# DLRM tower on one core: the last MLP layer as 64-wide parts on both halves of TensorE

## The reference

```
e = stack([tbl_f[ids[:, f]] for f in range(32)], axis=1)          # 1024 x 32 x 16
xk = e
for W in (W0, W1, W2):
    xk = relu(einsum('bmd,bhd,mhk->bkd', e, xk, W))               # 1024 x 64 x 16
    outs.append(sum(xk, axis=2))                                  # 1024 x 64
h = concatenate(outs + [dense_ctx], axis=1)                       # 1024 x 208
h = maximum(h @ W_top1 + b_top1, 0)                               # 1024 x 512
h = maximum(h @ W_top2 + b_top2, 0)                               # 1024 x 256
y = h @ W_top3                                                    # 1024 x 1
```

## Time and profile before

| | |
|---|---|
| median of 3 runs | 623.99 us (623.82 to 624.78) |
| the profiled execution, own time | 625.95 us |
| its span, first to last instruction | 624.0 us |
| TensorE busy | 600.8 us (96%) |
| VectorE, ScalarE, GpSimd busy | 515.1 (83%), 322.4 (52%), 444.2 us (71%) |
| granted TensorE clock, mean | 0.997 |

### The profile page before, as it was taken

The page is one execution under the profiler, slowest core; times in us unless marked ns, Lnnn a source line. Parts: engine busy times, 40 slices in busy tenths (PEclk is TensorE's granted clock), DMA queues, the critical chain, the costliest instruction groups (busy, mean ns, idle before and its releaser), DMA issues.

```text
span 624.0 us, 8470 instructions
## 1 busy us (share of the span) xinstructions
PE 600.8 (96%) x2926; PEld 211.4 (34%) x2926; DVE 515.1 (83%) x454; ACT 322.4 (52%) x545; POOL 444.2 (71%) x346
## 2 busy tenths in 40 slices
PE   4779899999999999999999999999999999999998
PEld 3532333333333333333333333333333333333454
DVE  0258698999989998999899998999899999888500
ACT  1333565555565454565545554545565456643564
POOL 6778858788787878787887878786878875556300
PEclk9999999999999999999999999999999999999999
DMA  4597787867887777677767887777667868750000
GB/s 128 184 333 257 283 308 292 285 239 258 274 283 274 258 244 253 222 289 246 258 227 282 283 275 245 252 283 253 222 236 265 289 242 273 269 197 0 1 1 0
DMA packets 45199, 144.49 MB, mean 232 GB/s; under 512 B 9619, under 2 KB 24085, under 8 KB 32870
## 3 DMA queue, kind: packets, MB, share of 16 engines
q1 hardware_dynamic: 36966, 141.85, 62.8%
q0 software_dynamic: 8192, 2.11, 4.0%
HBM read 139.21 MB, written 4.72 MB: 231 GB/s over the span
## 4 chain that ended last, share of the span: by engine, by line
PE 87%; POOL 5%; DMA 5%; issue 2%; SPq 1%; ACT 0%
PE acc L677 77%; POOL gathered L506 5%; PE x_ps L672 5%; DMA x_rows<-gathered 3%; PE sums_ps L746 2%; PE x_ps L746 2%; DMA gathered<-in_table,idx 1%; SPq L419 0%; DMA x_wide<-x_rows 0%; SPq L408 0%; DMA base_sb<-in_base 0%; PE sums_ps L672 0%; POOL idx L529 0%; ACT x_wide L593 0%; ACT x_wide L596 0%
## 5 line engine op out<-in xcount | busy, mean ns | idle before, releaser
L627 DVE TENSOR_TENSOR dve_ring<-x_wide,x_ps 128x1024 f32<-128x1024 f32 x428 | 489.2, 1215 | 62.2 <-issue 47.2
L677 PE MATMUL acc<-dve_ring,w_sb 128*64 128x512 f32 (+1 forms) x1744 | 474.6, 589 | 6.8 <-DVE dve_ring L627 6.8
L506 POOL DMA_INDIRECT gathered<-in_table,idx x256 | 243.8, 952 | 69.7 <-issue 64.1
L518 POOL TENSOR_TENSOR pool_ring<-x_wide,x_sb 128x1024 f32<-128x1024 f32 x84 | 199.3, 2383 | 76.7 <-ACT x_sb L577 46.9
L677 PEld LDWEIGHTS acc<-dve_ring,w_sb 128*64 128x64 f32 x1744 | 150.9, 138 | 293.4 <-issue 268.6
L677 PE MATMUL acc<-pool_ring,w_sb 128*64 128x512 f32 x336 | 131.6, 592 | 0.0
L567 ACT ACTIVATE x_ps<-acc 64x512 f32<-64x512 f32 (+1 forms) x132 | 73.5, 557 | 110.5 <-PE acc L677 108.2
L677 PE MATMUL acc<-pair_squares,w_sb 128*64 128x512 f32 (+1 forms) x264 | 113.9, 581 | 1.2 <-ACT pair_squares L547 1.2
L577 ACT COPY x_sb<-layer_out 64x512 f32<-64x512 f32 x128 | 79.0, 617 | 3.6
L547 ACT ACTIVATE pair_squares<-x_ps 128x1024 f32<-128x1024 f32 x32 | 32.8, 1025 | 88.5 <-PE sums_ps L672 88.2
L572 ACT ACTIVATE layer_out<-acc 64x512 f32<-64x512 f32 (+1 forms) x98 | 56.8, 579 | 2.4 <-PE acc L677 1.0
(11 more groups left out here) (36 smaller groups left out, 127.1 us busy)
## 6 DMA issues: line engine op xcount, KB each, us to landing
x_wide<-x_rows SPq DMA_DIRECT2D x96, 1024.0 KB, 8.0
x_wide<-x_rows SPq DMA_DIRECT2D x32, 768.0 KB, 5.6
x_wide<-x_rows SPq DMA_DIRECT2D x32, 256.0 KB
gathered<-in_table,idx POOLq DMA_INDIRECT x256, 4.5
x_rows<-gathered SPq DMA_DIRECT2D x32, 128.0 KB
w_sb<-in_w SPq DMA_DIRECT2D x2, 512.0 KB, 5.7
x_rows<-gathered SPq DMA_DIRECT2D x32, 16.0 KB
x_wide<-in_W_top SPq DMA_DIRECT2D x1, 512.0 KB, 4.3
```

What stands on the lines that cost most here:

```text
L506: pool.indirect_dma_start(gathered[:, c, j % 2, e * DIM:(e + 1) * DIM], None, table, bass.IndirectOffsetOnAxis(ap=idx[:, unit, e:e + 1], a ...
L518: nc.gpsimd.tensor_tensor(pool_ring[:, c], x0_step(c, j, layer, 2 * d, 2).rearrange("p (s n) -> p s n", n=COLS), x_sb[:, layer - 1, c, :]. ...
L627: nc.vector.tensor_tensor(dve_ring[:, c, slot:slot + width, :], x0_step(c, j, layer, i, width).rearrange("p (s n) -> p s n", n=COLS), x_ps ...
L677: done = nc.tensor.matmul(part, w, x[:, cols], start=first, stop=last)
```

## The change

The array `W_top3` that the host hands over becomes 128 x 2 x 64 with the real weight in column 0 and zeros in the 63 others, and `wt3` in SBUF grows with it. Layer 3 is now a product of 64 outputs like every other part, written to all 64 partitions of its half; ScalarE copies the first of them (partition 0 or 64).

With this, layer 3 can stand on either half. The plan puts (0, end) on half 1 ahead of (2, L2.1) and (2, L2.3), and leaves (1, end) and (2, end) on half 0, behind (2, L2.0) and (2, L2.2). A part of layer 3 is not planned earlier than the end of all layer-2 parts of its chunk (`until`).

```diff
@@ mlp_plan
+            (1, last[1], [(0, layer2[3])] + [(1, i) for i in layer1[1::2]] + [(2, i) for i in layer1[1::2]]
+             + [(1, i) for i in layer2[1::2]] + [(0, end)] + [(2, i) for i in layer2[1::2]]),
             (0, last[1], [(0, layer2[2])] + [(1, i) for i in layer1[0::2]] + [(2, i) for i in layer1[0::2]]
-             + [(1, i) for i in layer2[0::2]] + [(0, end)] + [(2, i) for i in layer2[0::2]] + [(1, end), (2, end)]),
-            (1, last[1], [(0, layer2[3])] + [(1, i) for i in layer1[1::2]] + [(2, i) for i in layer1[1::2]]
-             + [(1, i) for i in layer2[1::2]] + [(2, i) for i in layer2[1::2]])]
-    plan = []
+             + [(1, i) for i in layer2[0::2]] + [(2, i) for i in layer2[0::2]] + [(1, end), (2, end)])]
+    plan, until = [], {}
...
+            if i == end:
+                at = max([at] + [until[n, before] for before in layer2 if (n, before) in until])
             plan.append((at, one, half, n, i))
             at += steps * one
+            until[n, i] = at
@@ cin_tower
-        wt3 = mlp(H2 // P)
+        wt3 = mlp(H2 // P * HK).rearrange("p (c k) -> p c k", k=HK)
@@ hidden
-                    nc.scalar.copy(y_sb[:, first:first + rows], bank[0:1, 0:rows]).then_inc(hidden_made, 1)
+                    nc.scalar.copy(y_sb[:, first:first + rows], bank[half * HK:half * HK + 1, 0:rows]).then_inc(hidden_made, 1)
@@ mlp_step
-                    w, x, bank = wt3[:, k:k + 1], h2[:, k, cols], bank[0:1, :]
+                    w, x = wt3[:, k, :], h2[:, k, cols]
@@ kernel
-    arrays["W_top3"] = np.asarray(inputs["W_top3"]).reshape(-1, P).T
+    arrays["W_top3"] = np.zeros((P, H2 // P, HK), np.float32)
+    arrays["W_top3"][:, :, 0] = np.asarray(inputs["W_top3"]).reshape(-1, P).T
```

More of the change, by code:

```diff
@@ L153, in mlp_plan @@
             one = MLP_CHUNKS[n][1] / COLS
+            if i == end:
+                at = max([at] + [until[n, before] for before in layer2 if (n, before) in until])
             plan.append((at, one, half, n, i))
             at += steps * one
+            until[n, i] = at
     return sorted(plan)
 def mlp_done_order():
-    ends = [(at + one * (MLP_STEPS[MLP_PARTS[i][0]] - 1), at, n, i, half) for at, one, half, n, i in mlp_plan()]
-    return [(end + 1.2, n, i, half) for end, at, n, i, half in sorted(ends)]
+    ends = [(at + one * (MLP_STEPS[MLP_PARTS[i][0]] - 1), n, i, half) for at, one, half, n, i in mlp_plan()]
+    return [(end + 1.2, n, i, half) for end, n, i, half in sorted(ends, key=lambda part: part[0])]
 def in_order(works):
```

## The result

| | before | after |
|---|---|---|
| median, first comparison (7 runs each) | 624.78 us | 620.54 us |
| median, second comparison (18 and 12 runs) | 623.88 us | 621.59 us |
| ratio, first comparison | | 0.9947, 95% interval 0.9927 to 0.9968 |
| ratio, second comparison | | 0.9958, 95% interval 0.9946 to 0.9971 |
| profiled execution: own time, span | 625.95, 624.0 us | 622.79, 620.9 us |

The ratios are estimated from all executions and differ a little from the quotients of the medians (0.9932 and 0.9963). One of the 18 executions of the kernel before took 1627.06 us and is left out of the ratio.

What follows compares the result with a forecast made beforehand. TensorE was taken to bound the tail from 614.8 us. With its rows overlapped and a new wait, the last copy ends at 619.8 instead of 622.40, -2.6 us: median 623.99 to 621.4 us, range 620.7 to 622.5.

Steps and rivals of the forecast that it cites:

- The bound: TensorE holds 87% of the chain; only its tail changes, and 614.8 us of the span stay as they are.
- the sign of being wrong that I had named: Wrong altogether if the time before 614.5 moved, as with a late W_top3 or another pace of the interaction steps.
- The change-overs and the overlap: Tail on TensorE: no 1-wide visits, each costing some 0.24 us of change-over; short rows run beside (0, end), through by 616.6.
- B: Tail: long rows hold up the other half's short ones altogether, without change-over; no measurable change, 624.2 us; chance 0.06.
- C: Tail: as with no overlap of halves, plus 0.15 us drain at each of ten changes; slower, 625.7 us; chance 0.05.
- Strict order: Rival for the tail: each row waits for every earlier row to start; gain 1.7 to 1.9, 622.2 us; chance 0.15.
- the rule that I set against the trace: Trainium skill: TensorE products start and end strictly in program order; the forecast held three starts in the trace against it.
- The new wait: Ahead of (2, end)'s second step: TensorE idle about 0.7 us, as ScalarE copies chunk 1 before taking (2, L2.3) out.
- What was taken as nothing: Costs put at zero: 64-wide weight loads (137 ns against 82), W_top3 growing to 64 KB, ScalarE's copy from partition 64.

Runs made afterwards that it cites:

- layer2_first: Changed kernel with (0, end) moved behind (2, L2.1) and (2, L2.3) on half 1; start of last 384 row of (1, L2.3) to last copy's end: 5.31 us.

## Why the prediction was right

**The bound.** Nothing ahead of the tail moved: 502.7 us lie between the two marks in either kernel. The tail did begin 0.41 earlier, but so did the mark at 111.79 (111.38), so the sign of being wrong that I had named, another time before 614.5, came from the first 112 us. Reading the tail alone was right.

**The change-overs and the overlap.** Forecast: no 1-wide form, (0, end) through 1.7 us after half 1 comes free, short rows beside it. Measured: rows of 512 from 614.42, the last at 615.71 (that group's second row is already the first of (1, end)), and the next part of half 1 at 616.13, 1.71 later. The width alone gave 2.28 us, so this step is shown and not only argued. Rivals B and C fall with it: long and short rows are open together, and no gaps of 0.1 to 0.2 stand at the changes from long to short.

**Strict order** (rival A) did not happen: (2, L2.2) starts at 614.90, while the second step of (0, end), which stands ahead of it in the program, starts only at 615.28. But half of the rule that I set against the trace holds. (2, L2.2) has its last row in the group at 615.35 (four rows, the last open until 615.95), and stands behind (0, end) in the program, whose last row runs from 615.71 to 616.30. ScalarE's copy of chunk 0 waits until 34 parts are counted as done, and with the one taken out at 615.53 it was 33. Had (2, L2.2) been counted when its last row ended, it would have been the 34th at 615.95; ScalarE was idle on until 616.34, when (0, end) had ended. The trace records when that counter of parts is raised, and it says the same: at 615.50, 616.31 and 616.40, and not in between. So rows of different halves start out of program order and are reported in order. The Trainium skill, "TensorE: Matmul & The Clock Gate", Part 3, The mechanism, has both start and end in order; here the reported end agrees (616.31, 616.40) and the start does not (614.90 ahead of 615.28).

**The new wait.** Forecast: about 0.7 us without work for TensorE ahead of the last product, a copy of 0.47 ahead of what it waits for. Measured: two rows at 617.83 that end at 618.23, and the next two at 618.71, released by ScalarE, 0.47 later. The wait is there, but the chain into it was not mine. I had (1, end) wait behind the first step of (2, L2.1), which stands ahead of it in the program; its first row, in the group at 615.71, went ahead of that step (616.13). So it ran 0.3 earlier than I had put it: its last row starts at 616.96, 617.37 on the clock of the kernel before, where I had 617.7. What filled the time instead is ScalarE: from 616.34 it works without a pause through the copy of chunk 0, two layer-2 parts, the copy of chunk 1 and the part that the last product needs, to 618.57. I had counted only the last two. The copy of chunk 0 can't begin before (0, end) has ended, at 616.30, and ScalarE's fixed order puts all the others behind it. TensorE then took 0.14 to follow ScalarE (618.57 to 618.71) where I had 0.05. The end came out the same, 619.8 forecast against 619.40 + 0.41 = 619.81 on the clock of the kernel before; that these misses cancel, and the sum is right to 0.01, is luck.

**What was taken as nothing.** The 64 KB of W_top3 landed in 4.0 us where the 1 KB took 4.1. The copy from partition 64 takes 0.58 (616.34), as from partition 0 in the kernel before:

```profile
617.94 0.58 ACT L593 COPY x_wide<-sums_ps 1x512 f32<-1x512 f32 x1 [0.59 <-PE sums_ps L746]
```

The 64-wide weight loads, 137 ns, left the pace of 0.43 as it was.

**The size.** 2.6 in the sum, 2.59 in T and 0.1 behind it, which stood in the range. The first medians, 4.2 us apart, were not closer to the truth than the trace: the scatter of the first 112 us is as large as the gain. I had allowed a few tenths of a us for it; the seven executions of the changed kernel run from 619.29 to 623.93. That the first median fell 0.16 outside my range, and the second inside it, is within that scatter.

## What to carry to other kernels

A product that is narrow enough to be another form of the array (here 1 or 32 columns among products of 64) costs more than its rows: a visit cost some 0.24 us of change-over here and left the other half idle for its 0.86 us, so padding it with zeros to the width of its neighbours can be free of cost and give back both. Judge a change of a few us in a stretch by the stretch, from a row that both kernels share to the end, when the rest of the run scatters by as much. When a wait goes, write down every engine's queue behind it before putting a price on it: in layer2_first a bank and three copies took its place at once.

## What the runs showed of the hardware that was not expected

- The step between forms lies between 32 and 33 columns: T 8.81 and 5.29.
- Rows on the two halves start out of program order: all eight rows of (2, L2.2), 614.90 to 615.67, start ahead of the row of (0, end) at 615.71 that precedes them in the program. Their completions are reported in program order (ScalarE's 0.45 us of idle time up to 616.34 shows it).
- In ten executions of eight versions 502.7 us of TensorE's work repeat to within 0.012 us, while the 112 us ahead of them scatter by 4 (108.5 to 112.4).
- A copy of one partition of 512 numbers from PSUM took 0.68 us on VectorE and 0.58 on ScalarE.
